# Local attention of a four-layer kernel: sums over keys in two PSUM banks, three products halved on GpSimd, the values' bias in the output's bias, exponentials one step sooner

## The reference, cut to what matters

```
x = x + L0_attn_b_ref(layernorm(x))           # query (T=8 batches as time, 512 as batch, 256)

qkv = einsum('tbe,fe->tbf', query, in_proj_weight) + in_proj_bias
q, k, v = split(qkv);  q = q * scaling        # 16 heads of 16
dist = clip(s - t, -16, 16) + 16              # s, t run over only 8 positions here
scores = q.k + q.rel_pos_keys[dist]
probs = softmax(scores, over the 8 keys)
attn = sum over the 8 keys s of probs[t, s] * v[s]
return einsum('tbe,oe->tbo', attn, out_w) + out_b
```

## Time and profile before

| | us |
|---|---|
| median of 3 runs (lowest, highest) | 2650.02 (2644.34, 2658.11) |
| the profiled execution | 2654.06 |
| its span, first to last instruction | 2652.3 |
| PE busy, all of the span | 2465.1 (93%) |
| DVE, ACT, POOL busy | 1835.1, 1438.0, 1332.1 |
| second iteration of local attention, from 1577.66 to 1649.33 | 71.67 |

### The profile page before, as it was taken

One profiled execution on the slowest core, in us unless ns is written; L12 is line 12 of the kernel. 1 busy time (PEld: TensorE's weight loads), 2 busy tenths in 40 slices (PEclk: granted clock), 3 DMA queues, 4 the chain that ended last, 5 costly groups with the idle time before them and its releaser, 6 DMA issues. The chain is left out here.

```text
span 2652.3 us, 46652 instructions
## 1 busy us (share of the span) xinstructions
PE 2465.1 (93%) x15144; PEld 1430.2 (54%) x15144; DVE 1835.1 (69%) x3682; ACT 1438.0 (54%) x2991; POOL 1332.1 (50%) x1349
## 2 busy tenths in 40 slices
PE   6999999999999999989996899976999999989998
PEld 3555555554444444368886466652344444349897
DVE  5988999898788887843333457666778888844333
ACT  3666666666777777643332222113777777753332
POOL 5455666553345554246555466644235554445555
PEclk9999999999999999999998799988999999999999
DMA  5333333343434444145554000004434444335554
GB/s 161 94 109 97 109 108 101 106 117 101 121 113 126 126 130 120 53 150 193 195 177 155 22 1 17 17 24 133 120 109 131 129 129 121 94 113 168 195 195 137
DMA packets 249650, 305.92 MB, mean 115 GB/s; under 512 B 27746, under 2 KB 224577, under 8 KB 249412
## 3 DMA queue, kind: packets, MB, share of 16 engines
q1 hardware_dynamic: 237876, 275.37, 34.8%
q0 software_dynamic: 10176, 26.27, 2.8%
q10 hardware_dynamic: 1360, 1.31, 0.2%
HBM read 210.32 MB, written 92.84 MB: 114 GB/s over the span
## 5 line engine op out<-in xcount | busy, mean ns | idle before, releaser
L769 DVE TENSOR_REDUCE neg_max_af<-sc_af 128x1 f32<-128x512 f32 (+3 forms) x864 | 551.1, 663 | 109.5 <-PE sc_af L474 84.5
L690 ACT ACTIVATE prob_af<-sct_af 128x512 f32<-128x512 f32 (+1 forms) x864 | 484.5, 582 | 249.1 <-PE sct_af L495 137.4
L769 DVE TENSOR_REDUCE neg_max_f<-sc_f 128x1 f32<-128x512 f32 x512 | 334.0, 685 | 92.1 <-PE sc_f L474 90.1
L690 ACT ACTIVATE prob_f<-sct_f 128x512 f32<-128x512 f32 x512 | 291.0, 598 | 134.8 <-PE sct_f L495 133.0
L474 PE MATMUL sc_af<-stack_k_af,stack_q_af 96*128 96x512 bf16 (+3 forms) x1024 | 332.2, 345 | 19.3 <-DVE neg_max_af L769 13.4
L495 PE MATMUL sct_af<-stack_q_af,stack_k_af 99*128 99x512 bf16 (+3 forms) x1024 | 331.3, 346 | 5.2 <-ACT prob_af L690 4.4
L1598 PE MATMUL y_ps_e<-w_r,hT_e 128*128 x1120 | 258.5, 384 | 7.5 <-issue 5.6
L798 DVE SCALAR_TENSOR_TENSOR prob_af<-prob_af,w_r 128x512 f32<-128x512 f32 (+2 forms) x224 | 231.5, 1042 | 25.9 <-ACT prob_af L690 25.7
L526 PE MATMUL out_af<-prob_af,v_aug_af 128*32 128x512 f32 (+3 forms) x2048 | 232.3, 525 | 6.8 <-DVE prob_af L798 5.9
L1598 PEld LDWEIGHTS y_ps_e<-w_r,hT_e 128*128 128x128 f32 x1120 | 209.4, 192 | 38.4 <-issue 11.9
L495 PEld LDWEIGHTS sct_af<-stack_q_af,stack_k_af 99*128 99x128 bf16 x1024 | 100.1, 98 | 228.5 <-ACT prob_af L690 147.6
(11 more groups left out here) (373 smaller groups left out, 4744.7 us busy)
## 6 DMA issues: line engine op xcount, KB each, us to landing
w_r<-in_f_W_dram SPq DMA_DIRECT2D x66, 1024.0 KB, 5.0
stack_k_af<-k_parts_d SPq DMA_DIRECT2D x64, 384.0 KB, 4.2
k_parts_d<-parts_af SPq DMA_DIRECT2D x187, 128.0 KB
q_parts_d<-parts_af SPq DMA_DIRECT2D x96, 128.0 KB
stack_q_af<-q_parts_d SPq DMA_DIRECT2D x64, 192.0 KB, 3.0
stack_k_f<-k_parts_d SPq DMA_DIRECT2D x32, 384.0 KB, 4.3
w_next<-in_f_W_dram SPq DMA_DIRECT2D x12, 1024.0 KB, 4.9
k_parts_d<-parts_f SPq DMA_DIRECT2D x91, 128.0 KB
```

The source lines that it names most:

```text
L690: nc.scalar.activation(dst, src.rearrange("p (h q) -> p h q", h=len(heads)), ACT.Exp).then_inc(S.exp_done, 1)
L769: nc.vector.tensor_reduce(M.neg_max[:, qt, heads[0]:heads[-1] + 1], src, AX.X, ALU.max, negate=True).then_inc(S.max_done, 1)
```

## The change

`project_v` no longer adds the values' bias. Instead two more small loads bring that bias, DVE spreads it, PE multiplies it by the output weight at tile 17 of the experts, and DVE adds the product to the output's bias before this is split into its three parts. Queries 0, 1 and 2 of the first three tiles (`PRE_ADDED`) are halved by POOL: a second instruction adds keys 4 to 7 to keys 0 to 3 (128 x 1024), after a wait for its own product, and PE then sums 4 parts, not 8. Pairs of queries go to banks in turn: 0 and 1 to `att_ps`, 2 and 3 to `b_ps`, 4 and 5 to `att_ps` (in the last tile to `a_ps[0]`). DVE's own sums of queries 6 and 7 go to the PSUM bank `s_ps[0]`, `normalise` 3 reads them there and comes before `normalise` 2. ACT makes both exponentials one `read_projections` sooner, except in the last iteration. Semaphores of the input loads are joined.

```diff
 # experts: SP, then PE, then DVE
+                        sp.dma_start(bv[:, c:c + 1], A["b_b_in"][2 * D + P * c:2 * D + P * c + P].unsqueeze(1)).then_inc(L.params, 16)
...
+                    for o in range(DC):
+                        last = nc.tensor.matmul(rank_ps[:, D:2 * D], bv_wide[:, o, :], L.w_o[:, o, :], start=(o == 0), stop=(o == DC - 1))
...
+                        nc.vector.tensor_scalar(bv_wide[:, o, :], C.ones[:, :], bv[:, o:o + 1], None, ALU.mult).then_inc(L.rel_made, 1)
...
+                    nc.vector.tensor_tensor(bo_row[:, :], rank_ps[0:1, D:2 * D], bo_row[:, :], ALU.add).then_inc(L.rel_ready, 1)
...
+PRE_ADDED = [() if bt == NBT - 1 else (0, 1, 2) for bt in range(NBT)]
...
+    def sum_bank(bt, j):
+        if j == 1:
+            return b_ps
+        return a_ps[0] if bt == NBT - 1 and j == 2 else att_ps
...
 # PE, project_v
+                if t == 0 and bt >= 2:
+                    pe.wait_ge(normed, 4 * (bt - 2) + 2)
                 r0 = (NTM - 1 - t) * H
-                nc.tensor.matmul(b_ps[:, 0:D], ones3[:, :], bias3[:, 2 * D:3 * D], start=True, stop=False)
                 for c in range(DC):
-                    nc.tensor.matmul(b_ps[:, 0:D], xnT[:, c, t * P:t * P + P], w[:, c, 2 * D:3 * D], start=False, stop=(c == DC - 1))
+                    nc.tensor.matmul(b_ps[:, 0:D], xnT[:, c, t * P:t * P + P], w[:, c, 2 * D:3 * D], start=(c == 0), stop=(c == DC - 1))
...
 # PE, sum_over_keys
-                n = 3 * bt + t // 2
-                if t % 2 == 0 and n >= 1:
-                    pe.wait_ge(normed, 4 * ((n - 1) // 3) + (n - 1) % 3 + 1)
-                for s in range(NTM):
-                    last = nc.tensor.matmul(att_ps[:, D * (t % 2):D * (t % 2) + D], C.ident[:, :], buf[:, s * D:s * D + D],
-                                            start=(s == 0), stop=(s == NTM - 1))
+                j = t // 2
+                bank = sum_bank(bt, j)
+                if t % 2 == 0:
+                    if j == 1:
+                        pe.wait_ge(b_read, NTM * min(bt + 2, NBT))
+                    elif bt == NBT - 1 and j == 2:
+                        pe.wait_ge(dve_prod, dve_item(bt, DVE_QK[0], False) + 1)
+                    elif j == 2:
+                        pe.wait_ge(normed, 4 * bt + 1)
+                    elif bt >= 1:
+                        pe.wait_ge(normed, 4 * bt)
+                parts = NTM // 2 if t in PRE_ADDED[bt] else NTM
+                for s in range(parts):
+                    last = nc.tensor.matmul(bank[:, D * (t % 2):D * (t % 2) + D], C.ident[:, :], buf[:, s * D:s * D + D],
+                                            start=(s == 0), stop=(s == parts - 1))
...
 # ACT, iterations 0 to 2
                     read_projections(bt + 1, 3)
+                    exp(bt, 0)
                     read_projections(bt + 1, 4)
-                    exp(bt, 0)
                     read_projections(bt + 1, 5)
+                    exp(bt, 1)
                     read_projections(bt + 1, 6)
-                    exp(bt, 1)
...
 # DVE: sum_scores, own_values, normalise, order
+                    dve.wait_ge(normed, 4 * bt)
...
-                    if bt >= 1 and t == 6:
-                        dve.wait_ge(oT_made, 4 * bt)
-                    nc.vector.tensor_reduce(att[:, t, :], buf[:, :].rearrange("p (s c) -> p c s", s=NTM), AX.X, ALU.add).then_inc(own_summed, 1)
+                    dve.wait_ge(dve_prod, dve_item(bt, 3, True) + 1)
+                    nc.vector.tensor_reduce(s_ps[0][:, D * (t - 6):D * (t - 6) + D], buf[:, :].rearrange("p (s c) -> p c s", s=NTM), AX.X, ALU.add).then_inc(own_summed, 1)
...
+                src = (s_ps[0] if j == 3 else sum_bank(bt, j))[:, :].rearrange("p (t h e) -> p t h e", t=2, h=H)
...
+                normalise(bt, 3)
                 normalise(bt, 2)
-                normalise(bt, 3)
...
 # POOL, values
+                made = nc.gpsimd.tensor_tensor(split_heads(buf), v, weight[:, t, :, :].unsqueeze(3).to_broadcast(wide), ALU.mult)
+                if t in PRE_ADDED[bt]:
+                    made.then_inc(pool_step, 1)
+                    pool.wait_ge(pool_step, len(PRE_ADDED[0]) * bt + PRE_ADDED[bt].index(t) + 1)
+                    made = nc.gpsimd.tensor_tensor(buf[:, 0:4 * D], buf[:, 0:4 * D], buf[:, 4 * D:8 * D], ALU.add)
+                made.then_inc(pool_prod, 1)
```

More of the change, by code:

```diff
@@ L1499, in experts @@
     if L:
-        w_nat, bq_wide = sb("w_nat", [P, DC, D]), sb("bq_wide", [P, DC, P])
+        w_nat, bq_wide, bv, bv_wide = sb("w_nat", [P, DC, D]), sb("bq_wide", [P, DC, P]), sb("bv", [P, DC]), sb("bv_wide", [P, DC, P])
         bq, rel, head, rel_heads = sb("bq", [P, DC]), sb("rel", [P, NREL]), sb("head", [P, DC, H]), sb("rel_heads", [P, DC, NREL, H])
@@ L1622, in rel_products @@
                     pe.wait_ge(S.rank_sb, i_last + 1)
-                    pe.wait_ge(L.rel_made, 3)
+                    pe.wait_ge(L.rel_made, 5)
                     pe.wait_ge(L.params, NPARAM)
@@ L1632, in rel_products @@
                     for o in range(DC):
-                        last = nc.tensor.matmul(rank_ps[:, 0:NREL * H], bq_wide[:, o, :], rel_heads[:, o, :, :].rearrange("p r h -> p (r h)"),
-                                                start=(o == 0), stop=(o == DC - 1))
+                        nc.tensor.matmul(rank_ps[:, 0:NREL * H], bq_wide[:, o, :], rel_heads[:, o, :, :].rearrange("p r h -> p (r h)"),
+                                         start=(o == 0), stop=(o == DC - 1))
+                    for o in range(DC):
+                        last = nc.tensor.matmul(rank_ps[:, D:2 * D], bv_wide[:, o, :], L.w_o[:, o, :], start=(o == 0), stop=(o == DC - 1))
                     last.then_inc(L.rel_ps, 1)
@@ L1817, in prepare_local @@
                     dve.wait_ge(L.rel_ps, 2)
-                    nc.vector.tensor_copy(b_row[:, 3 * D:NB_COLS], rank_ps[0:1, 0:NREL * H]).then_inc(L.rel_ready, 1)
+                    nc.vector.tensor_copy(b_row[:, 3 * D:NB_COLS], rank_ps[0:1, 0:NREL * H])
+                    nc.vector.tensor_tensor(bo_row[:, :], rank_ps[0:1, D:2 * D], bo_row[:, :], ALU.add).then_inc(L.rel_ready, 1)
                 if s == 19:
@@ L1978 @@
 NB_COLS = 3 * D + NREL * H
-NPARAM = 16 * (5 + DC + 8)
+NPARAM = 16 * (5 + 2 * DC + 8)
 POOL_QK = (0, 1, 2, 3, 4, 5)
@@ L2037, in local_attention @@
     s_ps, att_ps = [psum("s0"), psum("s1")], psum("att")
-    x_half = sem("x_half")
-    x_loaded = [sem(f"x_loaded{i}") for i in range(NBT)]
+    x_half, x_rest = sem("x_half"), sem("x_rest")
+    x_loaded = sem("x_loaded")
     st_done, mv_done, var_done, rstd_done, shift_done, xn_ready = sem("st_done"), sem("mv_done"), sem("var_done"), sem("rstd_done"), sem("shift_done"), sem("xn_ready")
@@ L2044, in local_attention @@
     soft, shifted, weights_ready, inv_step, normed = sem("soft"), sem("shifted"), sem("weights_ready"), sem("inv_step"), sem("normed")
+    pool_step = sem("pool_step")
     oT_made, attT_ready, y_made, y_ready, stored = sem("oT_made"), sem("attT_ready"), sem("y_made"), sem("y_ready"), sem("stored")
@@ L2072, in _ @@
             sp.dma_start(x[0][:, 0:4, :], x_in[0][:, 0:4, :]).then_inc(x_half, 16)
-            sp.dma_start(x[0][:, 4:NTM, :], x_in[0][:, 4:NTM, :]).then_inc(x_loaded[0], 16)
+            sp.dma_start(x[0][:, 4:NTM, :], x_in[0][:, 4:NTM, :]).then_inc(x_loaded, 16)
             for bt in range(1, NBT):
-                sp.dma_start(x[bt][:, :, :], x_in[bt]).then_inc(x_loaded[bt], 16)
+                sp.dma_start(x[bt][:, :, :], x_in[bt]).then_inc(x_rest, 16)
             for bt in range(NBT - 1):
@@ L2214, in norm @@
                 act.wait_ge(shift_done, 3 if bt >= 1 else 1 if 0 in ts else 2)
-                if bt == 0 and 0 in ts:
+                if bt >= 1:
+                    act.wait_ge(x_rest, 16 * (NBT - 1))
+                elif 0 in ts:
                     act.wait_ge(x_half, 16)
                 else:
-                    act.wait_ge(x_loaded[bt], 16)
+                    act.wait_ge(x_loaded, 16)
                 if bt >= 1:
@@ L2406, in normalise @@
                     dve.wait_ge(pe_summed, len(PE_SUMS) * bt + 2 * j + 2)
-                    if bt >= 1:
-                        dve.wait_ge(oT_made, 4 * bt)
-                    src = att_ps[:, :].rearrange("p (t h e) -> p t h e", t=2, h=H)
                 else:
                     dve.wait_ge(own_summed, 2 * bt + 2)
-                    src = a
+                if bt >= 1:
+                    dve.wait_ge(oT_made, 4 * bt)
+                src = (s_ps[0] if j == 3 else sum_bank(bt, j))[:, :].rearrange("p (t h e) -> p t h e", t=2, h=H)
                 nc.vector.tensor_tensor(a, src, inv[:, ts, :].unsqueeze(3).to_broadcast([P, 2, H, HD]), ALU.mult).then_inc(normed, 1)
@@ L2423, in _ @@
             stats(1, range(4))
-            dve.wait_ge(x_loaded[0], 16)
+            dve.wait_ge(x_loaded, 16)
             stats(2, range(4, NTM))
@@ L2427, in _ @@
             shift_of(2, slice(4, NTM))
-            for bt in range(1, NBT):
```

(7 more changed lines are left out.)

## The result

| | before | after |
|---|---|---|
| median, first comparison | 2651.19 | 2615.9 (lowest 2610.77, highest 2623.87) |
| ratio, 95% interval | | 0.987 [0.9839, 0.9901] |
| median, second comparison | 2646.16 | 2610.03 |
| ratio, 95% interval | | 0.9858 [0.9837, 0.988] |
| profiled execution's span | 2652.3 | 2616.2 |

The change makes the kernel 1.3 to 1.4% faster: 35.3 and 36.1 us. The forecast was 2612.3, a gain of 37.7. The span of the profiled execution lost 36.1; the loop of local attention, from PE's first transposes to the transposes of the last output, went from 259.70 to 218.28, which is 41.4. Of the four executions of the kernel that the experiments call *no halves*, one took 5687.08 us, and the median and ratio given for it leave that one out.

The account below looks back on a forecast made before the run. PE was taken to set the period, each step off its queue counting one for one: 2.2 + 5.0 + 15.9 + 5.9 + 9.6 - 0.9 = 37.7 us, from median 2650.02 to 2612.3; range 2600 to 2629.

Parts of the forecast that it names:

- Step 1: Values' bias matmul out of `project_v`: 0.21 us per projection, 5.0 in iterations 0 to 2, 2.2 ahead of the loop.
- Step 2: Three queries summed by PE in 4 parts instead of 8: 5.3 us an iteration, 15.9 in three.
- covered by 0.3: First iteration: POOL has query 2 ready at +38.9, PE wants it at +39.2, so no wait.
- second rival: POOL's additions are slow, 3.2 or 4.5 us each: total 2614.5 to 2615, or 2621; chance 0.10.
- Step 3: Second bank for PE's sums removes waits for `normalise`: 1.96 us an iteration, 5.9 in three.
- Step 4: Last iteration: with three banks PE's sums wait for products only, four of them at full clock: 9.6 us gained.
- third rival: Low clock in the last iteration turns the 9.6 gain into a loss of up to 8.5: 2630; chance 0.10.
- Step 5: Added work: four records at the experts' tile 17 lose 0.9 us; loads, spreads, one-row addition and joined semaphores cost nothing.
- The exponentials: Start at +26.2 instead of +36.3 in ACT's queue, letting POOL's additions hide; no term of their own in the sum.
- covered by 4 us: DVE's second `own_products` ends at +62.3; PE needs it only for its second projection, over 4 us later.

Follow-up runs that it names:

- no halves: The changed kernel without POOL's halving, PE summing 8 parts of every query: steady iteration 66.06 us, loop 231.28, median 2624.51, ratio 0.989.
- four halves: The changed kernel with POOL also halving query 4 in tiles 0 to 2: steady iterations 59.15 us, last 48.47, median 2606.67, ratio 0.985.
- One bank: The changed kernel with all sums in one bank, each pair waiting for the normalise before it: steady iteration 63.43 us, median 2628.96, ratio 0.9915.
- second profiles: The kernel before and the changed kernel, each profiled once more unchanged: loop 258.41 and 217.44 us, spans 2648.1 and 2604.3.
- late exponentials: The changed kernel with both exponentials back in their old places: steady iterations 68.03 and 68.15 us, loop 238.06, median 2630.64, ratio 0.9924.

## Why the prediction was right, step by step

The bound was rightly named: PE alone sets the period of iterations 0 to 2, and each step taken from it counted in full. The period itself was forecast at 62.7 and is 60.88, mostly because one of the three steps was twice the size forecast. *No halves* and *four halves*, at 66.06 and 59.15, move by 1.73 a query. The three steps close: 3.27 (bias) + 5.18 (halves) + 2.55 (banks) = 11.0, against 71.67 - 60.88 = 10.8. The last two were taken out of the changed kernel, the first put into the one before, so they need not add up to better than that.

- Step 1, bias: right in kind, wrong in size. The term "8 x 0.21 = 1.7" an iteration measures 3.27, "5.0" in three measures 9.8 in steady terms. I took the step from the bias matmul's start to the next start for its cost, and left out the 0.1 on either side. Ahead of the loop, at a granted clock of 0.50 and with a wait of 0.58 in front, the step went from 4.35 to 4.02, as forecast.
- Step 2, halves: 15.9 forecast; 5.18 and 5.18 in the steady iterations, 3.8 to 4.6 in the first, where PE waits 0.48 for query 2, the place that the forecast called covered by 0.3. POOL's addition takes 2.35 (forecast 2.3, bounds 1.8 and 3.2), so the second rival fell. All nine additions take 2.35 to 2.37, beside DVE work with at most one operand in SBUF, and `normalise` 3 went from 1.00 to 0.69. The kernel before had a nearer row for them than the 1.58: the same L1052 takes 1.15, half of 2.3, at 1803.70, where DVE is idle beside the first half of it. It takes 1.58 at 1810.61, where DVE instructions with two operands in SBUF (L981, then L983) run beside all of it. The trace thus agrees with the Trainium skill (GPSIMD Engine Reference, 1. Specifications), which puts contention down to DVE instructions with two SBUF inputs. No 128x1024 addition stood beside such an instruction, so its price there is not shown.
- Step 3, banks: 1.96 forecast, 2.55 measured against the changed kernel with one bank. With halves the first wait ends at the same point of DVE's order and the second becomes longer.
- Step 4, last iteration: 9.6 forecast; 10.3 and, between the second profiles, 9.4. *One bank* shows 8.8 of it to be the banks'. Clock and order came as assumed; the third rival fell. The first two sums ran 9.5 us at a mean clock of 0.74 and the rest at 1.00.
- Step 5, what is added: 0.86 from 1310.75 to 1311.61 for the four records, 0.9 forecast. The four small loads end at 1220.3 in SP's queue, whose next entry is at 1223.7, so the two new ones are hidden.
- The exponentials: rightly given no term. They are cover: without them the halves turn into a wait, and 20 of the 41 us of the loop go.
- DVE: rightly given no term in the sum, but nearer than "covered by 4 us" sounds. One more halved query is enough to let it reach the last iteration late.

The sum was 2.2 + 5.0 + 15.9 + 5.9 + 9.6 - 0.9 = 37.7; the loop alone, forecast at 36.4, gained 41.4 and 41.0. The time gained 35.3 and 36.1, with intervals from 26 to 43 and from 32 to 43 us, which can't tell 37.7 from 41. That it came within 2.4 of the forecast is in part luck: the loop gained 4.6 to 5.0 more than forecast, the bias alone 4.8, and the scatter outside the loop, of that size, hides it.

## What to carry to other kernels

When one engine's queue sets the period, read each step from start to start of its neighbours with and without it, not from its own start to the next: a small bf16 matmul among fp32 ones cost 0.20 us more than its own step, which for 256 columns is twice the step. Before work is moved to an engine with slack, look when its input arrives. The halves paid only because the exponentials came 9 us sooner: with halves and late exponentials the iteration takes 68.03, longer than the 66.06 without any halves. And slack that recovers in a steady iteration doesn't recover in the last.

## What the runs showed of the hardware

- At a granted clock of 1.00, a bf16 matmul of 3 rows between fp32 matmuls of 128 costs its own step and 0.20 us more: 0.21 + 0.20 = 0.41 for 256 columns, 0.31 + 0.20 = 0.51 for 512.
- Behind a wait of 4.08 us on PE (*late exponentials*) the granted clock is 0.67, and 5.2 us of matmuls take 7.8. Behind one of 4.95 us (*one bank*, last iteration) two sums take 5.91 instead of 3.62.
- POOL's 128x1024 fp32 addition takes 2.35 beside DVE work with at most one SBUF operand. The 128x512 one of L1052 takes 1.15, and 1.58 where DVE instructions with two run beside all of it.
